# A four-layer graph network on one core: nine of 25 destination tiles get no adjacency and are summed by row gathers and one-hot products

## The chip, the core and the metric

The kernel runs on one core of one Trainium2 chip. The metric is the time of one execution on the device in microseconds (us), less is better. The five engines are called TensorE (PE in the profile; its weight loads PEld), VectorE (DVE), ScalarE (ACT), GpSimd (POOL) and SyncE (SP), which issues most of the DMAs.

## The reference, cut to what matters

There are N = 3125 nodes with 256 features and E = 53125 edges (50000 random ones and a loop for every node), sorted by destination. Four layers follow one another; each sums over the edges that arrive at a node, adds its input and normalises.

```
edge_index = stack([src, dst])
# layer 0: h = x @ W; deg = segment_sum(1, dst) + 1; norm = dinv[src] * dinv[dst]
#          out = relu(segment_sum(h[src] * norm, dst) + h * dinv**2 + b)
x = layernorm(x + L0(x))
# layer 1: agg = segment_sum(x[src] * edge_weight, dst); out = agg @ W_rel.T + b_rel + x @ W_root.T
x = layernorm(x + L1(x, edge_weight))
# layer 2: four heads of attention, a softmax over the edges of each destination
x = layernorm(x + L2(x))
# layer 3: out = relu(segment_sum((x @ W)[src] * edge_weight, dst) + b)
x = layernorm(x + L3(x, edge_weight))
```

## The kernel before

**Tiles.** The nodes are NT = 25 tiles of 128; the last holds 53. Every destination tile gets two dense adjacency matrices, sources by destinations: `ac`, the counts in bf16, used at once by layer 0, and `aw`, the weights in fp32 (1.6 MB for a tile), which is stored in `adjacency` in HBM and read back in layers 1 and 3. The random sources of a tile's some 2200 edges lie in all 25 source tiles, so that a matrix is [128, 25, 128].

**Prologue.** The edges are loaded, brought into a table of 16-edge rows (`edge_rows` in HBM), degrees are counted, and each node's row of `x @ W0` times `dinv` is split into three bf16 parts, `y0p` (semaphore `b_p3` counts the tiles that are done). SP issues its DMAs in order; among them are the `source_nodes` stores (L337, L339) in runs of 20 bytes.

**Layer 0, one tile per step `t`.** POOL's `edge_rows` gathers the tile's edges (one indirect DMA of 32 rows, one for each panel of four destinations), TensorE's `turn_fields` turns them, ScalarE's `digits` copies them to SBUF, VectorE makes one-hots of the sources (L801), of the destinations (L804) and three weighted ones (L809). TensorE's `adjacency(i, q)` multiplies them, eight quads `q` per tile (L1198, L1205); ScalarE's `counts` writes `ac` and VectorE's `add_weights` (L822) adds into `aw`. Then `aggregate` (L1213) multiplies `ac` with `y0p`: 25 blocks by three parts, 75 products of 256 columns, into `out_banks[t % 2]`, which three start products (L1251) had filled with the node's own row. The two banks alternate, so the sum of tile t (`sums0`, L839 on) may be taken during step t + 1. Each tile then passes `normalise` (L832, L833), `turn_x_next` (L1222), `relate` (L1231: the products with both weights of layer 1) and ScalarE's copy to `ybuf` (L553), one stage per step. VectorE makes the one-hots of the next tile in the second half of a step.

**Layers 1 and 3.** `dense(t)` (L1285; in layer 1 also `first_dense`, L1237, and `last_dense`, L1300; in layer 3 the first blocks ahead of time, L1451) multiplies the 25 blocks of the tile's weights with `ybuf` in fp32, while SP loads the next tiles (`load_a`, L345) into four slots. A slot's next load waits until its tile is done. Layer 1 adds two products per tile for the rows of the attention table (L1309).

**Layer 2.** 84 groups of 640 edges; for each, POOL gathers five times 128 rows of `attention_rows` (L483); VectorE, ScalarE and TensorE work out the softmax by windows of 48 destinations.

**Loops.** How many passes over edges a tile needs is worked out on the chip (`nswb`, from the fullest panel), and the steps are loops over it (`Fori`). Engines wait on counting semaphores; `sem_inc(held, 1)` stands behind some waits.

## Time and profile before

| | us |
|---|---|
| median of 3 runs | 1743.56 |
| lowest and highest | 1742.60 and 1746.69 |
| span of the profiled execution | 1741.4 |
| PE, DVE, ACT, POOL busy | 1579.5, 1180.5, 511.6, 520.9 |

The span runs from the first to the last instruction. In the page's 40 slices of 43.5 us the stages can be told by VectorE's digits: the prologue up to about 96 us, layer 0 up to 574, layer 1 up to 861, layer 2 from 871 to 1417, the rows of layer 3 up to 1484, layer 3 to the end.

```profile
## 2 busy tenths in 40 slices
PE   5879999999999999999868888888888879999998
DVE  9789999999997322122269999999999978211111
POOL 0032121221210200000077777777777700000000
PEclk9989999999999999999969999999999989999999
```

### The profile page before, as it was taken

The numbers are of one execution on the slowest core, as the hardware profiler recorded it, in microseconds if no ns is written. First come the engines' busy times: TensorE is split into PE (matmuls) and PEld (weight loads), VectorE is DVE, ScalarE is ACT, GpSimd is POOL, SyncE is SP. The second block draws the span as 40 slices with busy tenths as digits, with TensorE's granted clock in tenths as the row PEclk, the third lists the DMA queues.
The fourth block names the chain that finished last, engine by engine and source line by source line (L and its number), as shares of the span: only waits on it lengthen the run. The fifth ranks groups of instructions, "written<-read, shape, count | busy, mean of one in ns | idle before, by whom it ended". The sixth has DMA issues, their size and how long they took to land.

```text
span 1741.4 us, 37805 instructions
## 1 busy us (share of the span) xinstructions
PE 1579.5 (91%) x13731; PEld 1287.7 (74%) x13731; DVE 1180.5 (68%) x2739; ACT 511.6 (29%) x996; POOL 520.9 (30%) x540
## 2 busy tenths in 40 slices
PE   5879999999999999999868888888888879999998
PEld 4668787878877888888646666666666657888887
DVE  9789999999997322122269999999999978211111
ACT  0532322223222000000245555555555545000000
POOL 0032121221210200000077777777777700000000
PEclk9989999999999999999969999999999989999999
DMA  8912122122225244443144444444444441544440
GB/s 216 62 43 116 80 99 99 81 117 81 114 83 234 79 163 133 155 161 127 57 107 112 112 113 112 113 112 112 113 114 113 111 129 39 196 167 165 165 163 11
DMA packets 81220, 203.71 MB, mean 117 GB/s; under 512 B 42635, under 2 KB 57327, under 8 KB 71439
## 3 DMA queue, kind: packets, MB, share of 16 engines
q1 hardware_dynamic: 60047, 141.94, 26.0%
q0 software_dynamic: 20992, 59.37, 13.0%
q8 instruction: 113, 1.85, 0.4%
q14 instruction: 68, 0.56, 0.1%
HBM read 153.00 MB, written 53.57 MB: 119 GB/s over the span
## 4 chain that ended last, share of the span: by engine, by line
PE 59%; POOL 15%; DVE 11%; issue 11%; DMA 2%; ACT 1%; DVEq 0%; POOLq 0%; SPq 0%; ACTq 0%
PE bank L1285 29%; POOL ring L483 15%; PE bank L1213 10%; PE bank L1205 5%; PE bank L1198 3%; PE bank L1231 2%; PE bank L1397 2%; DMA ring<-attention_rows,work 2%; DVE work L809 1%; PE bank L1309 1%; DVE big L822 1%; PE bank L1149 1%; PE bank L1222 1%; PE bank L1115 1%; ACT work L608 1%
## 5 line engine op out<-in xcount | busy, mean ns | idle before, releaser
L483 POOL DMA_INDIRECT ring<-attention_rows,work x420 | 398.5, 949 | 149.2 <-issue 144.3
L1285 PE MATMUL bank<-big 128*128 128x256 f32 x1164 | 254.6, 379 | 0.0
L1285 PE MATMUL bank<-big,ring 128*128 128x256 f32 x1150 | 251.0, 379 | 0.0
L1397 PE MATMUL bank<-work,ring 128*65 128x48 f32 x3360 | 236.7, 231 | 12.7 <-ACT work L608 12.0
L1285 PEld LDWEIGHTS bank<-big 128*128 128x128 f32 x1164 | 220.2, 190 | 29.9 <-ACT big L632 0.4
L1397 PEld LDWEIGHTS bank<-work,ring 128*65 128x65 f32 x3360 | 225.9, 146 | 21.2 <-ACT work L608 19.4
L1285 PEld LDWEIGHTS bank<-big,ring 128*128 128x128 f32 x1150 | 217.6, 190 | 29.1
L1213 PE MATMUL bank<-big 128*128 128x256 bf16 x1875 | 209.0, 273 | 0.9
L1213 PEld LDWEIGHTS bank<-big 128*128 128x128 bf16 x1875 | 181.5, 98 | 25.3 <-ACT big L526 4.6
L608 ACT ACTIVATE work<-work 128x960 f32<-128x960 f32 x84 | 161.7, 1925 | 84.3 <-DVE work L1027 81.3
L822 DVE SCALAR_TENSOR_TENSOR big<-big,ring,bank 128x400 f32<-128x400 f32 x200 | 125.3, 628 | 34.1 <-PE bank L1205 27.2
L809 DVE TENSOR_TENSOR work<-work,ring 128x1600 bf16<-128x1600 bf16 x156 | 147.8, 986 | 0.0
L1205 PE MATMUL bank<-work 128*128 128x100 bf16 x2400 | 144.8, 209 | 0.0
L1096 DVE TENSOR_TENSOR u<-bank,bias 128x256 f32<-128x256 f32 x25 | 10.6, 425 | 193.7 <-PE bank L1285 193.7
L531 ACT ACTIVATE std<-mv,epsc 128x1 f32<-128x1 f32 x100 | 29.4, 294 | 345.1 <-DVE mv L828 344.5
L1380 PE MATMUL bank<-ident 128*32 128x512 bf16 x420 | 129.2, 408 | 0.0
L1372 PEld LDWEIGHTS bank<-ident,work 96*128 96x128 f32 x336 | 44.8, 193 | 107.5 <-DVE work L1008 105.3
L1205 PEld LDWEIGHTS bank<-work 128*128 128x128 bf16 x2400 | 122.7, 98 | 0.0
L1372 PE MATMUL bank<-ident,work 96*128 96x96 f32 x336 | 58.8, 298 | 64.8 <-DVE work L1008 64.5
L526 ACT CAST big<-bank 128x400 bf16<-128x400 f32 x200 | 96.6, 496 | 51.5 <-PE bank L1198 48.8
L446 POOL DMA_INDIRECT ring<-edge_rows,cur x26 | 24.8, 955 | 285.3 <-PE bank L1185 284.9
L994 DVE TENSOR_TENSOR work<-work,bank 128x960 f32<-128x960 f32 x84 | 96.2, 1145 | 1.3 <-issue 0.6
(220 smaller groups left out, 2050.4 us busy)
## 6 DMA issues: line engine op xcount, KB each, us to landing
adjacency<-big SPq DMA_DIRECT2D x25, 1600.0 KB, 5.1
ring<-adjacency SPq DMA_DIRECT2D x25, 1600.0 KB, 7.1
big<-adjacency SPq DMA_DIRECT2D x25, 1600.0 KB, 7.3
ring<-attention_rows,work POOLq DMA_INDIRECT x420
edge_rows<-edge_list SPq DMA_DIRECT2D x1, 4983.0 KB
x_sb<-in_x SPq DMA_DIRECT2D x1, 3072.0 KB
out_x<-xnT SPq DMA_DIRECT2D x24, 128.0 KB, 4.4
work<-attention_rows SPq DMA_DIRECT2D x168, 1.1 KB
```

The costliest lines, as they stand in the source:

```text
L483: G.indirect_dma_start(out=rows[0:EP, s, c, 0:ZG], out_offset=None, in_=ztab[:, :], in_offset=bass.IndirectOffsetOnAxis(ap=idx[:, g, c:c + ...
L526: S.copy(ac[:, :, q * QUAD * PAN:(q + 1) * QUAD * PAN], cnt_banks[q % 2][:, 0:NT * QUAD * PAN].rearrange("p (b d) -> p b d", b=NT)).then_i ...
L608: S.activation(prob[:, k % 2, :, :], val[:, k % 3].rearrange("p a c -> p c a"), ACT.Exp).then_inc(y["prob_ready"], 1)
L809: ins = V.tensor_tensor(oh[h][2][:, j], oh[h][1], repeated(digs[h][:, W1 + j], NT * PAN), ALU.mult)
L822: V.scalar_tensor_tensor(out=part, in0=part, scalar=keep[:, bass.ds(r, 1)], in1=w_banks[q % 2][:, 0:NT * QUAD * PAN].rearrange("p (b d) -> ...
L994: V.tensor_tensor(val[:, k % 3].rearrange("p (h w) c -> p h w c", h=H), pen[:, k % 3].unsqueeze(1).to_broadcast([EP, H, WIN, KC]), lg.rear ...
L1205: ins = mm(w_banks[b][:, 0:NT * QUAD * PAN].rearrange("p (b d) -> p b d", b=NT)[:, :, cols], lo[:, g, :, m], wtd[:, j, g, :, m].rearrange( ...
L1213: ins = mm(out_banks[t % 2][:, 0:D], ac[:, b, :], y0p[:, b, j, :], start=False, stop=False, skip_group_check=True)
L1285: ins = mm(bank[:, 0:D], slots[s][:, b, :], ybuf[:, b, :], start=(b == 0), stop=(b == NT - 1), skip_group_check=True)
L1372: ins = mm(mb_bank[:, j * 2 * WIN:(j + 1) * 2 * WIN], mg[:, j:j + 1].to_broadcast([2 * WIN, P]), ident[0:2 * WIN, 0:2 * WIN], start=True, ...
L1380: mm(bank[0:32, :].rearrange("p (a b) -> p a b", a=4), ident16[:, 0:32], columns, start=True, stop=True, skip_group_check=True)
L1397: ins = mm(sum_banks[k % 3][0:FH, h * WIN:(h + 1) * WIN], rows[0:EP, s, c, h * FH:(h + 1) * FH], prob[:, k % 2, c, h * WIN:(h + 1) * WIN], ...
```

## The change

Tiles 1, 4, 7, ..., 22 (eight of them, `SPARSE`) and the last, short tile 24 get no adjacency; the other 16 (`DENSE`) go through the steps as before, so layer 0 has 16 steps and layers 1 and 3 have 16 dense sums each. The edges of a sparse tile are cut in 18 chunks of 128 (8 for the last tile), in blocks of 10 and 8: 17 blocks and 152 chunks per layer. For each block SP loads the edges' sources and destinations (in layers 1 and 3 the weights too) as lists, POOL gathers 128 source rows per chunk from a table in HBM (`rows_layer0`, 1536 bytes a row; `rows_layer1`, `rows_layer3`, 1024 bytes), VectorE makes one-hots of destinations against the tile's 128 nodes (in layers 1 and 3 times the weight), and TensorE adds one-hot times rows: three bf16 products a chunk in layer 0, one fp32 product in layers 1 and 3.

The tables are new: SP stores `y0p` in five parts at the end of the prologue and each tile's rows in layers 1 and 3; six more stores keep the edge lists. In layer 0 there is now one bank for dense tiles and one for sparse ones, and one buffer for gathered rows and for one-hots; in layers 1 and 3 two of each. A block stands behind nearly every dense tile (`after0`: one per step, two in the last; `after1`: from step 1, two in steps 7 and 12; `after3`: from step 3, two in 5, 8, 11 and 13). Tiles leave layers in another order (`order0`, `order1`, `order3`). `nswb` now also covers the longest sparse tile. `edge_rows` copies its column of `cur` and `panel` first, since the tile is worked out in a register.

```
+    SPARSE = list(range(1, NT - 1, 3))
+    DENSE = [t for t in range(NT - 1) if t not in SPARSE]
+    halves = [Block(t, at, cnt, WIDE) for t in SPARSE for at, cnt in ((0, TEN), (TEN, WIDE - TEN))]
+    short = [Block(NT - 1, 0, SHORT, SHORT)]
+    blocks = short + halves + short + halves + halves + short
+    after0 = placed(0, [(k, 1 + (k == ND - 1)) for k in range(ND)])
+    after1 = placed(LAYER, [(k, 1 + (k in (7, 12))) for k in range(1, ND)])
+    after3 = placed(2 * LAYER, [(k, 1 + (k in (5, 8, 11, 13))) for k in range(3, ND)])
...
SP:
+            for table, whole, pad in ((esrc, src_e, pad_i[:, 0, :]), (edst, dst_e[:, 0:COLS], pad_i[:, 1, :]), (ew, w_e, pad_w)):
+                sp.dma_start(table[0:CAP].rearrange("(p e) -> p e", p=P), whole).then_inc(s_elist, 16)
+                sp.dma_start(table[CAP:CAP + P * WIDE].rearrange("(p e) -> p e", p=P), pad).then_inc(s_elist, 16)
...
+            for b in range(0, NT, 5):
+                sp.wait_ge(b_p3, b + 5)
+                sp.dma_start(y0tab[b * P:(b + 5) * P, :].rearrange("(t p) f -> p t f", p=P),
+                             y0p[:, b:b + 5].rearrange("p t j f -> p t (j f)")).then_inc(rows_stored[0], 16)
...
+            def lists(q):
...
+                    sp.wait_ge(chunk_done, two_blocks_back(nswb, q, r))
...
POOL:
+            def edge_rows(col, i):
                 pool.wait_ge(c_T, i + 1)
                 pool.wait_ge(c_next, i + 1)
                 pool.sem_inc(held, 1)
+                G.tensor_copy(cur1, cur[:, bass.ds(col, 1)]).then_inc(pool_col, 1)
+                G.tensor_copy(panel1, panel[:, bass.ds(col, 1)]).then_inc(pool_col, 1)
...
+            def gathers(q):
+                b, j = blocks[q], q % 2
                 with pool.Fori(0, nswb) as r:
+                    pool.wait_ge(lists_loaded[j], lists_here(nswb, q, r))
+                    if q >= LAYER:
+                        pool.wait_ge(chunk_done, two_blocks_back(nswb, q, r))
+                    pool.sem_inc(held, 1)
+                    for c in range(b.cnt):
+                        s = slot_of(q, c)
+                        if q < LAYER:
+                            pool.wait_ge(chunk_done, slot0_free(nswb, q, c, r))
...
+            edge_rows(DENSE[0], 0)
+            pool.wait_ge(rows_stored[0], 16 * (NT // 5))
+            pool.wait_ge(s_wz, 1)
+            for k in range(ND):
...
+                for q in after0[k]:
+                    gathers(q)
...
+            G.memset(big1[:, SPARSE_WORDS:], 0.0)
+            pool.wait_ge(rows_stored[1], 16 * NT)
+            for q in range(LAYER, 2 * LAYER):
+                gathers(q)
...
+            pool.wait_ge(chunk_done, blocks_done(nswb, 2 * LAYER - 1))
+            pool.sem_inc(held, 1)
+            G.memset(big1[:, 0:SPARSE_WORDS], 0.0).then_inc(acc_clear, 1)
...
VectorE:
+            def hots0(q):
+                b, pairs = blocks[q], blocks[q].cnt // PAIR
+                with dve.Fori(0, nswb) as r:
+                    relative(q, r, rel0, dst_l0)
+                    dve.wait_ge(chunk_done, rounds_done(nswb, q, r))
+                    V.tensor_tensor(hot0[:, 0:pairs], iota2.unsqueeze(1).to_broadcast([P, pairs, P, PAIR]),
...
+            def hots1(q):
+                b, j = blocks[q], q % 2
+                with dve.Fori(0, nswb) as r:
+                    relative(q, r, rel1[j], dst_l1)
+                    dve.wait_ge(chunk_done, two_blocks_back(nswb, q, r))
+                    for c in range(b.cnt):
+                        ins = V.tensor_scalar(hot1[:, j, c, :], iota_w[:], rel1[j][:, c:c + 1], w_l1[j][:, c:c + 1],
+                                              ALU.is_equal, ALU.mult)
...
+                for m in summed0(k - 1):
+                    normalise(e0, m, x_sb[:, order0[m], :])
+                for m in summed0(k)[:-1] if k < ND else summed0(k):
+                    sums0(m, k)
+                if k < ND:
+                    hots0(after0[k][0])
+                    sums0(summed0(k)[-1], k)
+                for m in summed0(k - 2):
+                    residual(m)
...
-                    dve.wait_ge(gathered[k % SLOTS], 16 * KC * uses(r, k))
+                    dve.wait_ge(gathered[k % SLOTS], 16 * KC * uses(r, k) + nswb * landed_before[k % SLOTS])
...
TensorE:
+            def scatter0(q):
...
+                with pe.Fori(0, nswb) as r:
+                    pe.wait_ge(hot_made, nswb * q + r + 1)
+                    for c in range(b.cnt):
+                        pe.wait_ge(rows_landed[slot_of(q, c)], nswb * (16 * slot_uses[q][c]) + r * 16 + 16)
+                        for j in range(3):
+                            ins = mm(sparse_bank[:, 0:D], hot0[:, c // PAIR, :, c % PAIR], rows0[:, c, j * D:(j + 1) * D],
...
+                        pe.wait_ge(rows_landed[s], landed)
+                        mm(bank[:, 0:D], hot1[:, q % 2, c, :], rows1[:, s, :], start=False, stop=False,
...
+            for k in range(ND + 3):
+                if k < ND:
+                    if k >= 1:
+                        pe.wait_ge(e0["u"], place0[DENSE[k - 1]] + 1)
+                    init0(dense_bank, DENSE[k])
...
+                relating, turning = summed0(k - 2), summed0(k - 1)
+                for m in relating[:1]:
+                    relate(m)
...
+                for m in turning[:1]:
+                    turn_x_next(e0, m, order0[m])
+                if k < ND:
+                    scatter0(after0[k][0])
+                for m in relating[1:]:
+                    relate(m)
...
```

## Rows read from the trace of the kernel before

**Rows 1.** The page's first line: the span and the instructions.
```profile
span 1741.4 us, 37805 instructions
```
**Rows 2.** Busy time by stage: layer 0, layer 2. The first line names the columns.
```profile
core 0: us, PE busy (x) PEld busy (x) DVE busy (x) ACT busy (x) POOL busy (x), PEclk, DMA share, GB/s
140.00:560.00 420.00, 409.02 (x4996) 338.04 (x4997) 385.55 (x587) 114.09 (x302) 82.77 (x88) 1.00 0.26 107
870.00:1417.00 547.00, 457.71 (x4788) 337.28 (x4788) 492.03 (x1262) 280.13 (x338) 398.46 (x420) 0.93 0.42 108
```
**Rows 3.** Timeline of one step: start us, us, engine, line, what, count, idle before.
```profile
284.21 0.50 PE L1251 MATMUL bank<-big,ident 128*128 128x256 bf16 x3
...
290.53 0.98 DVE L804 TENSOR_TENSOR work<-ring 128x1600 bf16<-128x1600 bf16 x1
...
291.61 8.36 PE L1213 MATMUL bank<-big 128*128 128x256 bf16 x75
...
299.81 1.88 PE L1231 MATMUL bank<-w_rr,xnT 128*128 128x512 f32 x4
...
301.11 0.15 DVE L832 RECIPROCAL rstd<-std 128x1 f32<-128x1 f32 x1
...
301.63 0.48 DVE L839 SCALAR_TENSOR_TENSOR u<-bank,dinv,bias 128x256 f32<-128x256 f32 x1
...
302.17 0.50 PE L1251 MATMUL bank<-big,ident 128*128 128x256 bf16 x3
...
303.16 0.39 DVE L847 TENSOR_TENSOR x_sb<-bank,x_sb 128x256 f32<-128x256 f32 x1
```
**Rows 4.** Prologue: SP's last long store, POOL after its first gather, two stretches.
```profile
45.65 39.12 SPq L339 DMA_DIRECT2D source_nodes<-in_src  x1
...
93.06 0.24 POOL L450 TENSOR_SCALAR cur<-cur 32x1 int32<-32x1 int32 x1 [20.07 <-DMA ring<-edge_rows,cur]
...
0.00:96.00 96.00, 62.53 (x609) 50.40 (x609) 79.49 (x195) 31.61 (x80) 8.86 (x15) 1.00 1.02 126
72.00:84.00 12.00, 9.05 (x45) 6.66 (x43) 9.50 (x28) 8.48 (x23) 0.99 (x1) 1.00 1.39 9
```
**Rows 5.** Timeline: the fields turned in the first step, and the second step's start.
```profile
110.14 0.41 PE L1185 MATMUL bank<-ident,ring 32*128 32x32 bf16 x5
...
123.08 0.49 PE L1251 MATMUL bank<-big,ident 128*128 128x256 bf16 x3
```
**Rows 6.** Timeline: first product of layer 1's second tile, last sum of layer 1.
```profile
573.88 10.96 PE L1285 MATMUL bank<-big 128*128 128x256 f32 x50
...
861.00 0.42 DVE L932 TENSOR_TENSOR u<-bank,x_sb 128x256 f32<-128x256 f32 x1 [7.56 <-PE bank L1300]
```
**Rows 7.** The chain that ended last: start us, us, what; in layers 1 and 3.
```profile
597.19 10.79 PE bank L1285 x50
...
1483.29 251.08 PE bank L1285 x1162
```
**Rows 8.** Two gathers of layer 2, one's landing in the chain, an adjacency store.
```profile
999.42 0.95 POOL L483 DMA_INDIRECT ring<-attention_rows,work  x1 [0.30 <-issue]
1000.67 0.94 POOL L483 DMA_INDIRECT ring<-attention_rows,work  x1 [0.30 <-issue]
...
1020.66 3.53 DMA ring<-attention_rows,work
...
adjacency<-big SPq DMA_DIRECT2D x25, 1600.0 KB, 5.1
```
**Rows 9.** Timeline: POOL and DVE instructions that overlap.
```profile
98.36 1.34 POOL L446 DMA_INDIRECT ring<-edge_rows,cur  x1 [0.18 <-issue]
...
273.48 1.22 DVE L801 TENSOR_TENSOR work<-ring 128x2048 bf16<-128x2048 bf16 x1
273.87 0.92 POOL L450 TENSOR_SCALAR cur<-cur 32x1 int32<-32x1 int32 x1 [1.67 <-DMA ring<-edge_rows,cur]
...
584.90 5.43 POOL L465 MEMSET big<- 128x6400 f32 x1 [56.44 <-PE bank L1285]
...
586.53 3.94 DVE L833 TENSOR_SCALAR x_sb<-u,mv,rstd 128x256 f32<-128x256 f32 x1
```

719 lines of the change are left out of this document (476 added, 243 removed).

## The prediction

> **What bounds the kernel now.** I read the page's span first [rows 1], then the table by stage [rows 2], then one period of layer 0 in the timeline [rows 3]. The four layers are limited by different things.
>
> Layer 0 (96 to 574 us) repeats every 17.96 us, once for each of 25 tiles: the start products of one step stand at 284.21, of the next at 302.17 [rows 3]. Follow two chains. TensorE goes from 284.21 through eight quads to 291.61, then 8.36 us of aggregation, 1.88 us of `relate`, a turn, and the next start. VectorE begins the one-hots at 290.53, is through at 301.11, normalises, sums, and releases that start. Both close at the same moment: the stage is balanced, 409 us of TensorE and 386 of VectorE busy in 420 [rows 2].
>
> Layers 1 and 3 are fp32 products back to back: 10.79 us for a tile of 25 blocks, and the whole end is one piece of 251.08 us [rows 7] (581 block products, two records each). One block product costs 251.08/581 = 0.432 us. Layer 2 (547 us [rows 2]) isn't touched; its gathers follow one another every 1.25 us [rows 8].
>
> **One pass or two.** All sparse work stands in loops over `nswb`. From the reference's inputs: the eight sparse tiles have at most 137 granules of 16 edges (144 fit 18 chunks), the last tile has 55 (64 fit), no panel has over 6. So `nswb` stays 1.
>
> **Layer 0, the period.** Twenty-five periods become 16, each with one block of 8 or 10 chunks (152 chunks in 17 blocks). Let D be the moment VectorE ends its one-hots. Two things become serial that weren't: the dense bank is now single, so TensorE's next start waits for `sums0` of this step, and `scatter0` stands ahead of that start and waits for `hots0`, which VectorE makes only after D.
> - Odd steps (block of 10, a sparse tile completed before): normalise 0.52 (301.11 to 301.63 [rows 3]), one more `sums0` 1.53 (301.63 to 303.16), list subtraction and one-hot of 1280 elements 1.35 (from 0.98 for 1600 elements, plus about 0.5 for the small instruction and two waits), 30 products of 8.36/75 = 0.111 us: 3.34, a second `relate` 1.88 and its wait: start at D+8.8.
> - Even steps (8 chunks): 1.04 + 1.25 + 2.7 + a second turn 0.4 (the one between 299.81 + 1.88 and 302.17): start at D+5.4.
> - From the start to the next D: 6.3 (284.21 to 290.53) + 10.6 (290.53 to 301.11).
> That gives 25.7 and 22.3, mean 24.0. Loop branches, a register wait ahead of every chunk and queueing behind POOL have no row; I bound them by 0 and 4 and take 1. Period 25.0. TensorE's own work is 22.6 (7.4 + 8.36 + 1.56 x 2.3 + 3.3), which would be the period if nothing were serial.
>
> POOL has to fit too: a gather every 1.25 us [rows 8] makes 11.3 us a step, and `edge_rows` about 8 (seven operations near 0.9, as L450's 0.92 [rows 9], and 1.7 of waiting): 19 of 25. Gathers start when the block before is consumed (D+4), the tenth lands 3.5 us after its issue (1020.66, 3.53 [rows 8]), near D+19; needed at D+27. Hidden with 8 us to spare; a store of the adjacency beside it takes some of that.
>
> **Layer 0, its ends.** Before it, `source_nodes` holds SP's queue to 84.8 (45.65 + 39.12 [rows 4]) and the engines are full of tiny packets: DMA share 1.39 at 9 GB/s between 72 and 84 us. The first row gather lands only at 93.06. The new store of `rows_layer0` (4.9 MB) stands behind all that, and POOL waits for its last part before its second `edge_rows`. An adjacency store (1.6 MB) lands in 5.1 us [rows 8], so 16 us at best; at the 126 GB/s of the first stage [rows 4] 39; I take 22 and its end at 118. Eight us of `edge_rows` later, at 126, TensorE can turn the fields that it turned at 110.14 before [rows 5]: +16, in which 3 us for six list stores and VectorE's dozen small instructions are counted. The first scatter and sum add 6. Start of step 1: 145 instead of 123.1 (+22; bounds +6 and +40).
>
> After it: D of step 15 is 145 + 14 x 25 + 16.9 = 512. Then the two last blocks and `first_dense` by the same prices: block 15 done at D+7, relate +1.9, 16 blocks at 0.432 (+6.9), the last 8 gathers free from D+4, landed D+17, scattered D+17.5; relate, 5 blocks, turns, three more relates with their ACT copies and 4 blocks: first dense product at D+33 = 545. Before: 573.88 [rows 6]. **Layer 0: -29** (period 22.6 and 28 give -63 and +13).
>
> **Layer 1.** Before, 573.88 to the last sum at 861.00 [rows 6] is 287.1: 24 x 10.79 [rows 7] + 28.1 for 25 tiles' inputs and turns. After: 15 x 10.79 = 161.9, 152 chunks x 0.432 = 65.7, the same 28.1, zero products and loops 6: 261.7. The first gathers can't start before the last row of layer 1 is stored: 4 + 10 + 2.5 against 11 of dense cover costs 5; later waits 3. So 269.7. Tail: two tiles are late together, and POOL clears 7760 words (5.43 us per 6400 [rows 9]: 6.6, mostly beside the last tiles' rows): +2. **Layer 1: -15.** The nine adjacency loads fewer save nothing by themselves: no product of the one piece of layer 3 [rows 7] waits for a load, and layer 1 is built alike.
>
> **Layer 2.** VectorE's `logits_sum` waits get one more register term, 84 times; no row. 0 to +4, I take +1. The stage between layers 2 and 3 gets only the stores of `rows_layer3`, on SP, where nobody waits for them before layer 3: 0.
>
> **Layer 3.** Before 251.1 [rows 7]. 43 blocks are done ahead in either. After: 357 x 0.432 = 154.2 + 65.7 + 6 = 225.9. But 152 gathers at 1.25 are 190 us, with only two blocks of buffer, and each block's lists and gathers may start only when the block two before is consumed. Laying the 17 blocks out by these prices gives 4 us of stalls at 1.25, 12 at 1.4, 20 at 1.5. I take 1.4: VectorE's 9 one-hots per block and the 1.6 MB loads get in the way. 240: **layer 3: -11**.
>
> **The shared port.** The trace shows POOL and VectorE waiting for each other: beside a memset of 584.90 + 5.43 a `tensor_scalar` that takes 0.41 took 3.94 and ended with it, and L450 (0.24 when free, 93.06 [rows 4]) took 0.92 and ended about when VectorE's one-hot of 273.48 did [rows 9]. The gather at 98.36 took 1.34 instead of 0.94, with the same two one-hot operations beside it. In layer 2 the gather's period stays 1.25.
> The Trainium skill, "SBUF — State Buffer", section "Who interferes with whom", says the second port pair of VectorE is GpSimd's only one and is locked exclusively for an instruction, by `tensor_scalar` in a two-port mode among others, and that DMAs issued by GpSimd starve meanwhile. `hots1` is made of nothing but `tensor_scalar`. By that rule 9 of them hold up each block's gathers in layers 1 and 3; with the page's own 3.1 us for a DMA issue that is overlapped instead of 0.62 the change would lose. Rows 9 agree for memset and small operations; for gathers no run here shows it beyond the 1.34.
>
> **Sum.** -29 - 15 + 1 - 11 = -54. The profiled execution's 1741.4 lies 2 us under the median of 1743.56, which carries over: 1743.56 - 54 = **1690 us**.
>
> **Rivals.**
> - *Full overlap* (0.12): waits shorter than laid out, period 22.6, TensorE's sum. Layer 0 gives -63: 1656. For: before, TensorE is 97% busy in this stage. Against: hots0 after D can't start earlier.
> - *Longer hand-over* (0.20): each of the new waits costs some 0.5 more, period 28: layer 0 +13, in all 1732. For: three hand-overs between VectorE and TensorE per step where there was one.
> - *Dear gathers* (0.12, slower): POOL's gather is held up in layers 1 and 3 behind `hots1`. At 1.75 us each layer 3 stalls 48 us (+22) and layer 1 13 (-8); with layer 0 the sum is near -15; from about 1.8 on the change costs time, and at 1.9 (layer 1 +11, layer 3 +44) it is 1771. Against: layer 2's steady 1.25 beside a VectorE that is 90% busy.
> - *Dear gathers and longer hand-over, both small* (0.05): within 0.3% of before, about 1743.
> - *Two passes* (0.01): excluded by the counts above; every adjacency would be built twice, over 2000.
> - The forecast, 0.50, with its own range 1665 to 1714.
>
> **Numbers.** 1690. Range 1650 to 1735, from full overlap to the longer hand-over with its bound; outside are mostly the dear gathers. Within 0.3% is about what a measurement of this kernel can tell from no change. Faster: 0.50 + 0.12 + 0.20 = 0.82; same 0.05; slower 0.13.
>
> **What would show it.** Start products of layer 0 every 25 us, in pairs near 23 and 27, with TensorE idle ahead of the scatter products for VectorE's one-hot. Fields of step 0 turned near 126. First full dense product near 545. In layer 3 POOL's gathers nearly unbroken, every 1.4 us, products waiting after the steps with two blocks. Wrong if the gather's period passes 1.7, if layer 0's period passes 28, or if TensorE waits for landed rows in layer 0.

## The result

The changed kernel takes 1673.92 us (median of 4 runs, 1669.85 to 1676.1) against 1743.08 for the kernel before: a ratio of 0.9601, with a 95% interval of 0.9581 to 0.962, or 69 us less. The prediction was 1690 (1650 to 1735), 54 us less. The profiled execution took 1676.1, its span is 1674.3 against 1741.4 [rows 1].

Busy time by stage of the changed kernel: the steady part of layer 0, layer 1, the end of layer 3. Columns as in rows 2.

```profile
core 0: us, PE busy (x) PEld busy (x) DVE busy (x) ACT busy (x) POOL busy (x), PEclk, DMA share, GB/s
140.00:470.00 330.00, 300.49 (x3429) 247.48 (x3427) 259.80 (x423) 78.69 (x198) 248.13 (x224) 0.99 0.48 158
524.00:804.00 280.00, 262.25 (x1210) 224.70 (x1208) 124.34 (x441) 25.95 (x113) 156.57 (x156) 0.98 0.50 161
1430.00:1667.00 237.00, 226.73 (x1032) 195.51 (x1030) 91.09 (x313) 7.44 (x25) 145.21 (x152) 0.99 0.56 183
```

Layer 0 was balanced between TensorE and VectorE before, each 92 to 97% busy [rows 2]. Now TensorE is busy 91% of it, VectorE 79%, and POOL, once at 20%, is at 75%: a third engine has come up close. Layer 2 is the same: 525.1 us from its first gather to its last in both kernels.

One step of layer 0 in the changed kernel (timeline, columns as in rows 3; L1569 starts a bank, L1063 is VectorE's first one-hot for the next tile, L1538 the dense aggregation, L1125 the block's one-hots `hot0`, L1583 the scatter products):

```profile
281.85 0.49 PE L1569 MATMUL bank<-big,ident 128*128 128x256 bf16 x3
...
288.05 0.99 DVE L1063 TENSOR_TENSOR work<-ring 128x1600 bf16<-128x1600 bf16 x1
...
289.14 8.36 PE L1538 MATMUL bank<-big 128*128 128x256 bf16 x75
...
298.62 0.15 DVE L1091 RECIPROCAL rstd<-std 128x1 f32<-128x1 f32 x1
...
301.24 0.83 DVE L1125 TENSOR_TENSOR ring<-ring 128x1280 bf16<-128x1280 bf16 x1 [0.20 <-DVE ring L1117]
...
302.27 3.45 PE L1583 MATMUL bank<-ring 128*128 128x256 bf16 x30 [2.10 <-DVE ring L1125]
305.56 1.88 PE L1556 MATMUL bank<-w_rr,xnT 128*128 128x512 f32 x4
307.28 0.49 PE L1569 MATMUL bank<-big,ident 128*128 128x256 bf16 x3
```

A step of 25.43 us, from 281.85 to 307.28. TensorE has nothing to do from 300.17 to 302.27: `hot0` stands behind VectorE's one-hots, which end at 298.70, and behind the sums. The wait for `hot0` is 2.1 and 1.2 us in turn over layer 0, 16 waits and 27.2 us in all. Dense tiles start at 138.50, 164.95, 186.93, 212.40 and so on to 472.11: alternately every 25.45 and 22.0 us, 23.83 on average (333.61 in 14 steps). Sixteen such steps stand where 25 of 17.96 stood [rows 3].

The start of layer 0 (timeline; L1510 turns the edge fields, L634 opens the second `edge_rows`, which waited for the stored rows):

```profile
103.36 0.82 PE L1569 MATMUL bank<-big,ident 128*128 128x256 bf16 x3
...
111.08 2.26 POOL L634 COPY ring<-cur 32x1 int32 x1 [12.01 <-DMA rows_layer<-big]
...
118.72 0.37 PE L1510 MATMUL bank<-ident,ring 32*128 32x32 bf16 x5 [1.97 <-POOL ring L649]
...
138.50 0.49 PE L1569 MATMUL bank<-big,ident 128*128 128x256 bf16 x3
```

The fields were turned at 110.14 and the second step began at 123.08 before [rows 5].

Both ends of layer 1 (timeline; L1656 dense products, L667 gathers, L697 the clearing on POOL, L1214 a cast and L1232 the last sum on VectorE, L709 the first gather of layer 2):

```profile
524.35 10.96 PE L1656 MATMUL bank<-big 128*128 128x256 f32 x50
...
532.88 0.95 POOL L667 DMA_INDIRECT big<-rows_layer,big  x1 [22.96 <-issue]
...
550.84 9.44 PE L1656 MATMUL bank<-big,ring 128*128 128x256 f32 x43
...
796.07 6.56 POOL L697 MEMSET big<- 128x7760 f32 x1 [12.90 <-PE bank L1604]
...
797.04 5.61 DVE L1214 CAST work<-edf 128x4 bf16<-128x4 f32 x1 [1.48 <-ACT edf L806]
...
803.84 0.42 DVE L1232 TENSOR_TENSOR u<-bank,x_sb 128x256 f32<-128x256 f32 x1 [0.38 <-issue]
...
817.99 0.95 POOL L709 DMA_INDIRECT ring<-attention_rows,work  x1 [15.36 <-issue]
```

Layer 1 takes 279.5 us from 524.35 to its last sum, against 287.1 [rows 6]. It loses at both ends: the first block's rows come so late that the next dense product starts 26.5 us after the first (10.96 of products and some 6 of scatter and inputs fill it), and the last sum stands behind a cast of four elements that takes 5.61 us, as long as POOL's memset runs.

In layer 3 TensorE stands before the scatter products that follow a step with two blocks (timeline; L507 issues a load of 1.6 MB of the adjacency):

```profile
1556.06 3.62 PE L1604 MATMUL bank<-big 128*128 128x256 f32 x16
1556.14 0.33 SPq L507 DMA_DIRECT2D big<-adjacency  x1
...
1563.33 1.57 PE L1604 MATMUL bank<-big 128*128 128x256 f32 x4 [3.66 <-DMA big<-rows_layer,big]
```

Where the time went, by stage (start and end read from the timelines):

| stretch | before | changed | difference | predicted |
|---|---|---|---|---|
| to the second step of layer 0 | 123.1 | 138.5 | +15.4 | +22 |
| second step to layer 1's first full dense product | 450.8 | 385.9 | -64.9 | -51 |
| layer 1 to its last sum, and on to the first gather of layer 2 | 297.2 | 293.6 | -3.6 | -15 |
| from that gather to the end of the stage before layer 3 | 612.2 | 612.9 | +1 | +1 |
| layer 3 | 251.1 | 236.3 | -15 | -11 |
| all | | | -67 | -54 |

### The profile page after: what moved, and what is told of

Read it like the earlier page. It is cut to its first block, busy times and chain, and to the rows that moved or that the text cites. A ratio compares the mean times of both kernels' runs of the same rounds, so it can differ in the third digit from the quotient of the medians.

```text
span 1674.3 us, 36559 instructions
## 1 busy us (share of the span) xinstructions
PE 1451.5 (87%) x12043; PEld 1166.7 (70%) x12043; DVE 1163.9 (70%) x2961; ACT 482.0 (29%) x906; POOL 1007.3 (60%) x1011
## 3 DMA queue, kind: packets, MB, share of 16 engines
q1 hardware_dynamic: 87087, 110.47, 22.3%
## 4 chain that ended last, share of the span: by engine, by line
PE 38%; DVE 19%; POOL 19%; issue 15%; DMA 6%; ACT 2%; DVEq 1%; SPq 0%; POOLq 0%; ACTq 0%
POOL ring L709 16%; PE bank L1656 15%; PE bank L1604 7%; DVE work L1068 5%; PE bank L1583 3%; PE bank L1530 2%; POOL big L667 2%; PE bank L1757 2%; DMA big<-rows_layer,big 2%; DMA ring<-attention_rows,work 2%; DVE big L1081 2%; DVE work L1063 2%; PE bank L1665 1%; PE bank L1474 1%; PE bank L1523 1%
## 5 line engine op out<-in xcount | busy, mean ns | idle before, releaser
L709 POOL DMA_INDIRECT ring<-attention_rows,work x420 | 398.4, 949 | 143.0 <-issue 139.1
L667 POOL DMA_INDIRECT big<-rows_layer,big x304 | 289.6, 953 | 288.9 <-issue 268.7
L663 POOL DMA_INDIRECT ring<-rows_layer,ring x152 | 196.3, 1291 | 66.1 <-issue 44.0
L1656 PE MATMUL bank<-big,ring 128*128 128x256 f32 x800 | 177.0, 382 | 0.0
L1656 PEld LDWEIGHTS bank<-big,ring 128*128 128x128 f32 x800 | 153.7, 192 | 21.6
L1604 PE MATMUL bank<-big 128*128 128x256 f32 x608 | 143.9, 390 | 17.8 <-DMA big<-rows_layer,big 17.8
L1656 PE MATMUL bank<-big 128*128 128x256 f32 x664 | 145.9, 379 | 0.0
L1604 PEld LDWEIGHTS bank<-big 128*128 128x128 f32 x608 | 114.8, 194 | 39.1 <-DMA big<-rows_layer,big 23.3
L1656 PEld LDWEIGHTS bank<-big 128*128 128x128 f32 x664 | 126.1, 190 | 17.6 <-ACT big L877 0.4
L1538 PE MATMUL bank<-big 128*128 128x256 bf16 x1200 | 133.8, 273 | 0.5
L1538 PEld LDWEIGHTS bank<-big 128*128 128x128 bf16 x1200 | 116.1, 98 | 16.1 <-ACT big L758 2.8
L1081 DVE SCALAR_TENSOR_TENSOR big<-big,ring,bank 128x400 f32<-128x400 f32 x128 | 80.0, 629 | 53.2 <-PE bank L1530 49.1
L1068 DVE TENSOR_TENSOR work<-work,ring 128x1600 bf16<-128x1600 bf16 x102 | 96.5, 988 | 0.0
```

Source lines behind the costliest of these rows:

```text
L663: G.indirect_dma_start(out=rows0[:, s, :], out_offset=None, in_=y0tab[:, :], in_offset=bass.IndirectOffsetOnAxis(ap=src_l0[j][:, c:c + 1], ...
L667: G.indirect_dma_start(out=rows1[:, s, :], out_offset=None, in_=(y1tab if q < 2 * LAYER else y3tab)[:, :], in_offset=bass.IndirectOffsetOn ...
L709: G.indirect_dma_start(out=rows[0:EP, s, c, 0:ZG], out_offset=None, in_=ztab[:, :], in_offset=bass.IndirectOffsetOnAxis(ap=idx[:, g, c:c + ...
L1068: ins = V.tensor_tensor(oh[h][2][:, j], oh[h][1], repeated(digs[h][:, W1 + j], NT * PAN), ALU.mult)
L1081: V.scalar_tensor_tensor(out=part, in0=part, scalar=keep[:, bass.ds(r, 1)], in1=w_banks[q % 2][:, 0:NT * QUAD * PAN].rearrange("p (b d) -> ...
L1538: ins = mm(dense_bank[:, 0:D], ac[:, b, :], y0p[:, b, j, :], start=False, stop=False, skip_group_check=True)
```

## The experiments

Every profile here is of one run. "Period" is the mean over the 14 steps of layer 0 from the second dense tile to the last.

| kernel | second step | period | layer 1's first dense product | from there to layer 2's first gather | median us | ratio to before (95%) |
|---|---|---|---|---|---|---|
| changed | 138.5 | 23.83 | 524.4 | 293.6 | 1673.9 | 0.9601 (0.9581 to 0.962) |
| e0, the same again | 137.2 | 24.41 | 531.4 | 290.7 | 1676.6 | 0.9607 (0.9587 to 0.9626) |
| e1 `hot0` first | 139.8 | 23.80 | 529.2 | 290.0 | 1674.1 | 0.9579 (0.9542 to 0.9615) |
| e2 gaps | 139.7 | 25.42 | 548.0 | 292.0 | 1696.4 | 0.9706 (0.9683 to 0.9728) |
| e3 lists first | 141.1 | 23.94 | 528.0 | 286.0 | 1677.3 | 0.9608 (0.9583 to 0.9632) |
| e4 clearing split | 139.6 | 23.99 | 528.9 | 284.2 | 1674.7 | 0.9574 (0.9542 to 0.9605) |
| e5 = e1 + e2 | 135.7 | 22.68 | 503.0 | 288.4 | 1651.4 | 0.9456 (0.944 to 0.9473) |
| e6 joints | 132.5 | 23.90 | 518.8 | 279.1 | 1664.7 | 0.954 (0.9517 to 0.9562) |
| e7 = e5 + e6 | 131.8 | 22.73 | 500.4 | 281.0 | 1641.8 | 0.939 (0.9366 to 0.9415) |
| e8 = e7, one gap | 131.4 | 22.32 | 493.2 | 280.8 | 1637.9 | 0.9394 (0.9378 to 0.941) |
| e9 = e7, copying spread | 128.7 | 22.70 | 496.5 | 280.8 | 1638.4 | 0.9402 (0.9384 to 0.9421) |
| e10 = e7 without layer 3's rows | 132.1 | 22.72 | 500.2 | 279.0 | 1625.0 | 0.9321 (0.9304 to 0.9338) |
| e11 = e8 + e9 | 127.6 | 22.30 | 489.8 | 278.0 | 1633.0 | 0.9366 (0.9342 to 0.9389) |

My theory of the period was that the hand-over `hot0` to scatter sets it. The first two runs test that, and what stands next in line.

**e1, the block's one-hots at the head of the step.**

```diff
+                    hots0(after0[k][0])
                     with dve.Fori(0, nswb) as r:
...
                 if k < ND:
-                    hots0(after0[k][0])
                     sums0(summed0(k)[-1], k)
```

> Edit: in layer 0 the one-hots of the sparse block (`hot0`) are made at the head of the step, ahead of the dense tile's adjacency, instead of behind its one-hots and sums (valid where each tile has one round, as here). In the changed kernel TensorE stood 2.10 us before the scatter products of 15 of the 16 steps, released by that `hot0` instruction. Theory A, the hand-over alone sets the period: init of the dense bank then comes every 21.9 us on average (alternately 23.4 and 20.0 to 20.9, some of the gain lost because VectorE starts its first weighted sum 1 us later) instead of 23.83; layer 0 is 23 to 31 us shorter and the kernel takes 1643 to 1651 us against 1674. Theory B, GpSimd is the next bound (edge rows 8 us and 9 gathers of 1.25 us on average is 19.3, plus a hold of 5.8 us in most steps is 22.5 to 25): the period stops at 22.8 or more, TensorE now waits for landed rows, and the kernel takes 1655 to 1665 us.

The waits for `hot0` (27.2 us in all; the 2.10 us that I had for 15 of the 16 steps hold for every second one) are gone, and nothing is gained that the timing shows: the period is 23.80 instead of 23.83. Timeline of a step with ten chunks in e1:

```profile
291.98 6.79 POOL L663 DMA_INDIRECT ring<-rows_layer,ring  x1 [0.30 <-issue]
...
299.34 2.47 PE L1583 MATMUL bank<-ring 128*128 128x256 bf16 x21
302.32 0.50 PE L1583 MATMUL bank<-ring 128*128 128x256 bf16 x3 [0.52 <-DMA ring<-rows_layer,ring]
...
304.74 0.51 PE L1583 MATMUL bank<-ring 128*128 128x256 bf16 x3 [0.65 <-DMA ring<-rows_layer,ring]
```

The last three rows come one by one, at the gathers' own pace, because one gather before them took 6.79 us instead of 0.95 (a hold, from here on). In the changed kernel such a hold is seen in 10 places in layer 0 and delays TensorE once, by 1.8 us in the first step; in e1 it comes in every step from the second on, and TensorE waits for landed rows 21 times between 140 and 480 us, 14.8 us in all. Theory B names the right mechanism; its size (1655 to 1665) was too kind. The slack that I had called 8 us was used up by the hold.

**e2, gaps in VectorE's one-hots.**

```diff
+            def one_hot_lo(h, i=None):
+                V.tensor_tensor(oh[h][0], numbers(P), repeated(digs[h][:, LO], P), ALU.is_equal).then_inc(c_lo, 1)
+                if i is not None:
+                    dve.wait_ge(c_lo, i * 2 + (h + 1))
...
+                else:
+                    ins.then_inc(c_wt, 1)
+                    if h == 1:
+                        dve.wait_ge(c_wt, i * 4 + (2 * h + j + 1))
...
-                        one_hot_code(1)
-                        one_hot_lo(1)
+                        one_hot_code(1, i + 1)
+                        one_hot_lo(1, i + 1)
```

> Edit: in layer 0 VectorE waits for the completion of each of the five one-hot instructions of the second half before it starts the next, so that its unbroken stretch (some 4.8 us of 2-input tensor_tensor on SBUF operands) is broken by four gaps of about 0.2 us. In the changed kernel a GpSimd instruction takes 6.3 to 6.9 us instead of 0.95 about once in every second step, and each time it ends where this stretch of VectorE ends. Theory A, the stretch holds the port that GpSimd's instruction needs and any gap lets it in: the longest GpSimd instruction of layer 0 drops to under 3 us, none of over 5 us is left. Theory B, the hold is of another origin (the DMA's descriptors, an instruction fetch): the 6 to 7 us instructions stay. Both: the hold is hidden behind GpSimd's slack, so the time doesn't fall; VectorE's own stretch is 1 us longer per step, the time is within -3 and +15 us of 1674.

The hold itself, first in the changed kernel (timeline; L1063, L1060 and L1068 are one-hots, `tensor_tensor` operations with both inputs in SBUF, the last five of which are the second half; L1081 is `add_weights`, with one input in PSUM; the last one-hot ends at 298.70):

```profile
288.95 1.22 DVE L1060 TENSOR_TENSOR work<-ring 128x2048 bf16<-128x2048 bf16 x1
289.18 1.81 POOL L663 DMA_INDIRECT ring<-rows_layer,ring  x1 [0.30 <-issue]
290.08 0.62 DVE L1081 SCALAR_TENSOR_TENSOR big<-big,ring,bank 128x400 f32<-128x400 f32 x1
...
292.07 1.89 DVE L1068 TENSOR_TENSOR work<-work,ring 128x1600 bf16<-128x1600 bf16 x2
292.73 6.79 POOL L663 DMA_INDIRECT ring<-rows_layer,ring  x1 [0.30 <-issue]
293.87 0.98 DVE L1063 TENSOR_TENSOR work<-ring 128x1600 bf16<-128x1600 bf16 x1
...
295.91 2.79 DVE L1068 TENSOR_TENSOR work<-work,ring 128x1600 bf16<-128x1600 bf16 x3
```

and in e2:

```profile
199.81 2.94 POOL L664 DMA_INDIRECT ring<-rows_layer,ring  x1 [0.30 <-issue]
...
200.94 0.98 DVE L1066 TENSOR_TENSOR work<-ring 128x1600 bf16<-128x1600 bf16 x1
...
201.96 1.23 DVE L1061 TENSOR_TENSOR work<-ring 128x2048 bf16<-128x2048 bf16 x1
```

Every hold of 6.3 to 6.9 us is gone; the longest is 3.04, a shade over the 3 expected. In both kernels POOL's instruction ends 0.8 us after the end of the one-hot operation that closes an unbroken train of them: 299.52 after 298.70, and 202.75 after 201.93, where the added wait leaves 0.04 us free before the next. What ends the train need not be a pause. At 298.70 VectorE had already begun its next instruction (L1091, of another form), and the gather of 289.18 ends at 290.99, 0.8 us after the one-hot of 288.95, though `add_weights` follows that at once (20 gathers of the changed kernel between 140 and 460 us end so, 0.77 to 0.83 us after such a one-hot). So the 6.79 us are the rest of one one-hot operation and the six behind it, the last of the first half included, and a gap or an operation of another form lets POOL in. That is theory A for the cause. For the time I was wrong: by the ratios (0.9706 against 0.9601) it is 18 us more, not at most 15. VectorE's five operations take 5.32 us instead of 4.82, not 1 us more, `hot0` is later by it, and TensorE's granted clock is 0.92 to 0.97 in most stretches of 50 us of layer 0 where it was 1.00; the period went from 23.83 to 25.42. How much of the 1.6 us is the clock's no run separates.

**e5, both edits together.**

> Edit: both edits of e1 and e2 together, `hot0` at the head of the step and a wait for completion after each one-hot instruction of the second half. In e1 TensorE no longer waited for `hot0` but for landed rows, and GpSimd had a hold of 6.79 us in every step; in e2 the longest hold was 3.0 us, but TensorE stood longer before the scatter products and its granted clock fell to 0.92 to 0.97 in most stretches of 50 us. Theory A, holds on GpSimd are the bound of e1: with both edits the holds are 3 us, TensorE waits for rows under 5 us in all of layer 0, dense tiles follow each other every 22.0 to 22.8 us and the first dense product of layer 1 comes at 500 to 512 us; the kernel takes 1650 to 1662 us. Theory B, the steps of e1 are bound by the gathers as such (a slot is free only when its last rows are multiplied): the period stays at 23.4 to 24 us, 1672 us or more.

Theory A holds in all its numbers: period 22.68, first dense product at 503.0, 1651.4 us. The first edit gains nothing alone, the second costs 18 us alone, and together they gain 25 (1651.4 against e0's 1676.6 on the same chip). TensorE now goes from `relate` straight into the scatter products (timeline of e5), and the table of the stretch shows it busy 95% at full clock:

```profile
334.62 0.50 PE L1578 MATMUL bank<-big,ident 128*128 128x256 bf16 x3
335.03 3.45 PE L1592 MATMUL bank<-ring 128*128 128x256 bf16 x30
338.32 1.88 PE L1565 MATMUL bank<-w_rr,xnT 128*128 128x512 f32 x4
...
140.00:480.00 340.00, 322.65 (x3666) 266.97 (x3663) 282.68 (x458) 83.70 (x212) 238.15 (x238) 1.00 0.52 170
```

**e8, one gap in place of four.**

```diff
+                if h == 1:
+                    ins.then_inc(c_lo, 1)
...
                         one_hot_code(1)
                         one_hot_lo(1)
+                        dve.wait_ge(c_lo, i + 2)
                         for j in range(3):
                             weighted(i + 1, 1, j)
```

> Edit: e7 with one wait for completion in VectorE's stretch of the second half (behind its second one-hot instruction) in place of four. In e5 and e7 the holds on GpSimd are 1.9 and 2.9 us, longer than one piece of VectorE's stretch (0.9 to 1.2 us), and TensorE stood 0.9 us in 14 steps before a transpose that waits for VectorE. Theory A, GpSimd's instruction gets in at the first gap: with one gap the holds are at most 4 us, VectorE is 0.5 us earlier in each step, the first dense product of layer 1 comes at 490 to 500 us instead of 500.4 and the kernel takes 1633 to 1642 us. Theory B, it needs more than one gap (2.9 us is two or three pieces): holds of 5 us or more are back, TensorE waits for landed rows as in e1, the dense product comes at 508 us or later and the kernel takes 1648 us or more.

The longest hold is 4.08 us (230.55 to 234.63; the operation before the one gap of that step ends at 233.80: again 0.8 later). Period 22.32, layer 0 shorter by 7 us in the profile. The ratio, 0.9394, can't be told from e7's 0.939, so the gain in the profile is shown for layer 0 only.

**e0, the changed kernel again.** Layer 0 ended 4 us later in e3 and e4, whose layer 0 is the changed kernel's, so I looked at how it scatters.

> The changed kernel itself once more, beside the next three on one chip, to see how far layer 0 alone scatters from run to run (its first dense product came at 524.35 us in the first profile, and at 528.0 and 528.9 in two kernels whose layer 0 is the same). Both theories: ratio to before 0.958 to 0.962. Theory A, the scatter is one of the start (TensorE's clock and the first step, 138.5 or 139.6 to 141.1 at the second dense tile) and of single steps: the first dense product lies between 523 and 530 us here. Theory B, the placement of code did it: it lies at 524.4 within 0.5 us.

The first dense product came at 531.4, a microsecond beyond theory A's bracket and 7 behind the first profile. The same step in both (timeline; the changed kernel first, then e0, then e0's table by stretch):

```profile
207.39 3.45 PE L1583 MATMUL bank<-ring 128*128 128x256 bf16 x30 [2.14 <-DVE ring L1125]
```
```profile
204.82 5.10 PE L1583 MATMUL bank<-ring 128*128 128x256 bf16 x30 [2.10 <-DVE ring L1125]
```
```profile
204.00:206.00 2.00, 1.18 (x6) 0.85 (x7) 1.90 (x5) 0.00 (x0) 0.69 (x1) 0.71 0.01 2
206.00:208.00 2.00, 2.00 (x11) 1.35 (x10) 0.46 (x2) 0.29 (x1) 1.01 (x3) 0.50 0.00 0
```

The same 30 products after the same wait of 2.1 us for `hot0` take 3.45 us in one run and 5.10 in the other, where TensorE's granted clock fell to 0.50, its lower level of 1.2 GHz, as it began them. What the engine had done before was the same by the rows: 8.36 us of products, 1.88, a turn, a start, then the wait. So the wait for `hot0` has a second price, which some steps of some runs pay, here 1.65 us. In e5, where the wait is gone, every stretch of layer 0 from 140 us on has a clock of 1.00, and its five runs lie within 3.9 us (1648.94 to 1652.83) where the changed kernel's lie within 7.6 in e0.

**e3, the lists of layer 1 first.**

```diff
             load_a(slots1[1], 1, 1)
+            lists(after1[1][0])
             sp.wait_ge(c_oh, nswb * (2 * ND) + 2)
...
-                for q in after1.get(k + 1, []):
+                for q in after1.get(k + 1, []) if k else []:
                     lists(q)
```

> Edit: at the start of layer 1 the edge lists of its first sparse block are loaded ahead of two adjacency loads, the last y1 stores and the load of the node indices, instead of behind them. In the changed kernel the first gather of layer 1 starts at 532.9 us, 5 us after its lists were issued and 9 us after the last y1 store was, and the first sparse block ends at 549.9 where TensorE alone would have ended it at about 540.5. Theory A, the lists' place in the queue sets the first gather: it starts 5 to 7 us earlier (right behind the last y1 store's landing), the first sparse block ends 5 to 8 us earlier, and the kernel takes 1666 to 1669 us. Theory B, the loads of 1.6 MB next to the gathers set when rows land (8.6 us was seen against 2.9): the gathers start earlier but the block ends less than 2 us earlier, 1672 to 1674 us.

The first gather comes 1.9 us after the first dense product instead of 8.5, and the third tile's products start 19.6 us after it instead of 26.5: theory A within layer 1. The time doesn't show it (0.9608, and 1677.3 us where I expected at most 1674): in its profile layer 0 was 3.7 us longer than in the changed kernel's, and so was the stretch from layer 2's first gather to the end. The scatter of e0 is as large as the gain.

**e4, the clearing cut in two.**

```diff
-            pool.wait_ge(chunk_done, blocks_done(nswb, 2 * LAYER - 1))
+            pool.wait_ge(chunk_done, blocks_done(nswb, 2 * LAYER - 2))
             pool.sem_inc(held, 1)
-            G.memset(big1[:, 0:SPARSE_WORDS], 0.0).then_inc(acc_clear, 1)
+            G.memset(big1[:, 0:TEN * D], 0.0)
+            G.memset(big1[:, 2 * TEN * D:2 * TEN * D + TEN * P], 0.0)
+            pool.wait_ge(e1["split"], 5 * NT)
+            pool.sem_inc(held, 1)
+            G.memset(big1[:, TEN * D:2 * TEN * D], 0.0)
+            G.memset(big1[:, 2 * TEN * D + TEN * P:SPARSE_WORDS], 0.0).then_inc(acc_clear, 1)
```

> Edit: the clearing of the 7760 words of rows and one-hots at the end of layer 1 is cut in two: one half behind the last block but one, the other behind VectorE's last split of a layer-1 tile. In the changed kernel that memset starts on GpSimd at 796.07 and takes 6.56 us, and VectorE's cast of 4 elements that starts at 797.04 takes 5.61 us instead of 0.16; the last sum of layer 1 comes behind it. Theory A, the memset holds VectorE: without it there the last sum starts 5 to 6 us earlier, the first attention gather too (at 812 to 813 instead of 818.0), and the kernel takes 1668 to 1669 us. Theory B, something else is as late (the scatter products, the stores of z): the first gather moves by under 2 us, 1672 to 1674 us.

Timeline of e4:

```profile
807.80 2.23 POOL L701 MEMSET big<- 128x2560 f32 x1 [18.46 <-DVE ring L1219]
...
813.07 0.97 POOL L714 DMA_INDIRECT ring<-attention_rows,work  x1 [1.81 <-issue]
```

No cast takes over 0.2 us there any more, though a copy beside the second clearing still takes 1.91 us (808.18) for 0.20. From the last scatter product to the first gather of layer 2 it is 14.5 us (798.6 to 813.1) instead of 22.1 (795.9 to 818.0). Theory A at its place; the ratio, 0.9574, is 5 us under the changed kernel's, within the interval, and the median of 1674.7 us is not the 1668 to 1669 expected. Layer 3 alone, the same in all kernels here but e10, takes between 236.2 (e8) and 242.6 us (this one) in their profiles, so that single gains of this size drown in the total.

**e6, three joints at once**: e3, e4, and POOL's wait for the stored rows behind the second `edge_rows` instead of ahead of it.

```diff
-            pool.wait_ge(rows_stored[0], 16 * (NT // 5))
             for k in range(ND):
...
                              if following > this else this, nswb * k + r + 1)
+                if k == 0:
+                    pool.wait_ge(rows_stored[0], 16 * (NT // 5))
```

> Edit: three moves at the joints, and layer 0's steps left as they are: e3's (lists of layer 1 first, 7 us shorter from the first dense product to the third in its profile), e4's (clearing cut in two, 7.5 us shorter from the last scatter product to the first attention gather), and GpSimd's wait for the layer-0 rows moved behind the second tile's edge rows, which don't need them. Theory A, the three gains are in series on the path: the first step of layer 0 is 5 to 8 us shorter (init of the second dense tile at 131 to 134 us instead of 138.5), from there to the first attention gather it is 14 us less, and the kernel takes 1650 to 1658 us, 18 to 24 us under the changed kernel on the same chip. Theory B, what is gained at one joint is waited for at the next (the DMA queues, the clock after it): under 8 us gained, 1667 us or more.

Each local number is as theory A had it: second step at 132.5, 279.1 us from the first dense product of layer 1 to layer 2's first gather (14.6 less than in the changed kernel, 11.7 less than in e0). The median fell by 12 us on the same chip (0.954 against 0.9607), less than the 18 to 24 expected. The profiled run was the fastest of its five, 7 us under the median; what the others lost, and where, I can't say without their profiles.

**e7, all of it.**

> Edit: everything of e1 to e4 and the moved wait of e6 together. Theory A, the gains add: e6's 20 us and e5's 12 to 22 us give 1630 to 1642 us. Theory B, layer 0 stays bound by GpSimd's gathers and only the joints gain: 1650 to 1660 us.

1641.8 us: at the upper end of theory A. e5's gain of 25 and e6's of 12 add to 37; measured 35 (0.939 against 0.9607 is 38 by the ratio).

**e9, the copying of the source nodes spread over layer 0.**

```diff
-            sp.dma_start(src_all[:, 0:FULL, :], src[0:FULL * EP * KC].rearrange("(g p k) -> p g k", p=EP, k=KC)).then_inc(
-                s_srcs, 16)
...
             for k in range(ND):
...
                 lists(after0[k][0])
+                lo, hi = FULL * k // ND, FULL * (k + 1) // ND
+                sp.dma_start(src_all[:, lo:hi, :], src[lo * EP * KC:hi * EP * KC].rearrange(
+                    "(g p k) -> p g k", p=EP, k=KC)).then_inc(s_srcs, 16)
```

> Edit: e7 with the copying of the source nodes (55 us of SyncE's queue in pieces of 20 bytes, ahead of the stores of layer 0's rows) cut into 16 parts that follow the list loads of layer 0's 16 steps, 3.4 us of the queue in each. In the changed kernel five stores of rows (960 KB each) start together at 91.6 us and the last lands at 111. Theory A, the queue's hold sets the first gathers: the row stores go out as their tiles are ready, the last lands at 104 to 108 us, init of the second dense tile comes 3 to 6 us earlier than in e7 (131.8), and the kernel takes 1636 to 1640 us on e7's scale. Theory B, the first step is bound by the edge rows and by the last tile of rows anyway, and 3.4 us of tiny pieces in each step only delay lists and adjacency stores: init of the second dense tile moves by under 1.5 us, 1640 to 1650 us.

The second step starts at 128.7, 3.1 us before e7's, and stays so to the first dense product (3.9). The last store of rows lands at 101.2, 9.9 us before e7's, so most of that is not on the path. Each of the 16 parts holds SP's queue for 0.6 to 1.7 us, 11.0 us in all, not for the 3.4 that I had divided out of 55: cut up, the copying holds the queue less. The ratio (0.9402) can't be told from e7's.

**e11, e8 and e9 together.**

> Edit: e7 with both e8's single wait and e9's spread copying of the source nodes. In the profiles of e8 and e9 the first dense product of layer 1 came 7.2 and 3.9 us earlier than in e7, while the medians of the three kernels were within what the timing tells apart (0.9390, 0.9394, 0.9402 of before). Theory A, both gains are real and the medians only scatter: the first dense product comes at 487 to 492 us and the ratio is 0.932 to 0.937 (1626 to 1634 us). Theory B, what is gained in layer 0 is given back later (the hand-over to layer 1, TensorE's clock): the ratio stays at 0.938 to 0.941 (1636 to 1642 us).

Theory A: the first dense product at 489.8, a ratio of 0.9366, though its interval still overlaps those of e7 and e8. This is the fastest complete kernel found, some 42 us under the changed one (0.9366 against 0.9607). It is valid as long as each tile has one round: with two, by the order of the waits (no run has two), `hot0` at the head of the step would wait for products that stand behind VectorE's own next one-hots.

**e10, layer 3 without its rows.**

```diff
-            for q in range(2 * LAYER, 3 * LAYER):
-                gathers(q)
...
-                        pe.wait_ge(rows_landed[s], landed)
+                        if e is not e3:
+                            pe.wait_ge(rows_landed[s], landed)
```

> Left out: layer 3's gathers, and the waits for their rows; the products run on what lies in the buffers, so the output is not the reference's. Otherwise e7. In e7 as in the changed kernel TensorE stood 10.4 us in layer 3 before scatter products, released by gathered rows that landed. Theory A, these landings are all that layer 3 loses: it is 9 to 12 us shorter from its first dense product to the end and the kernel takes 1630 to 1633 us on e7's scale. Theory B, the adjacency loads (16 of 1.6 MB) or VectorE's one-hots are next and as late: under 4 us gained.

From its first dense product with weights in `ring` to its last product layer 3 takes 217.9 us instead of e7's 237.1: 19.2 less, twice what theory A gave. The waits for landed rows are 10.4 us of that. The rest is in the same products (grouped by line and shape, e7 first; L1672 and L1671 dense, L1620 and L1619 scatter):

```profile
L1672 PE MATMUL bank<-big,ring 128*128 128x256 f32 x400 | 91.7, 392 | 0.0
L1620 PE MATMUL bank<-big 128*128 128x256 f32 x304 | 72.5, 391 | 10.5 <-DMA big<-rows_layer,big 10.4
```
```profile
L1671 PE MATMUL bank<-big,ring 128*128 128x256 f32 x400 | 87.5, 379 | 0.0
L1619 PE MATMUL bank<-big 128*128 128x256 f32 x304 | 67.9, 379 | 0.0
```

4.2 and 4.6 us, 8.8 in all: e7's granted clock in this stretch is 0.96, e10's 1.00. With the waits the clock's share goes too; the edit takes the gathers away together with the waits, so which of the two held the clock down is not shown. e7's profile is one of the dear ones: e8 and e9, whose layer 3 is e7's, take 232.9 and 233.8 us for the same stretch at a clock of 0.99, so that e10 is 15 to 16 us shorter than these, some 10 of waits and 5 of clock. By the timed ratios the gain is 12 us (0.9321 against 0.939); from layer 2's last gather to the first use of its sums e10's profile had 25.5 us, e7's 22.8. With no gathers TensorE is busy 221.97 of 222 us, so neither the adjacency loads nor VectorE's one-hots are next.

## Why the prediction was right, and where it wasn't

The direction, the stages and most mechanisms held, but that the sum came within 15 of the 69 us is in part luck. By the profiles layer 0 gained 20.5 us more than forecast (6.6 of them at its start) and layer 3 some 4 more, and layer 1 gained 11 less, which hid half of the first error.

- **Two hand-overs made serial set layer 0's period**: right. The layout gave 25.7 and 22.3 us; measured 25.45 and 22.0. The microsecond that I added for loops and register waits isn't there: 30 scatter products with ten waits take 3.45 us, where 30 x 0.111 is 3.34. Fourteen steps of it were the largest miss: 16 us. The layout's own hand-over is right to 0.3 us: D comes 16.9 us after the start, as laid out, and the next start 8.6 after D, laid out as 8.8.
- **Start, 145**: measured 138.5. The stores were mis-sized: POOL was let go at 111.1, not 118, as the five stores (4.9 MB) went out from 91.6 on and had all landed at 110.5: 256 GB/s from 91.6 to 111, where the 126 of the slow end would have taken 39 us. The first start product was 7 us later than before, where I had 3. Then 7.6 us of `edge_rows`, as said.
- **Hand-over to layer 1**: 52.2 us from the last start product to the first dense product, predicted 49.9.
- **Layer 1, 269.7**: measured 279.5. The term that failed is the waits, 8 in the sum. The first block cost about 10 (e3: the lists stood behind other loads, 7 of it), the later ones 1.3, and the clearing held VectorE for 5.6 just before the last sum (e4). I had the memset in the sum, from rows 9 even its power over VectorE, but "mostly beside the last tiles' rows", when the last sum was behind it.
- **Layer 2, +1**: measured nothing that stands out (525.1 us from first to last gather in both).
- **Layer 3, 240**: 236.3. The size was about right (225.9 and the 12 of stalls for a period of 1.4 make 238, not 240; measured stalls are 10.2), the place too, and the mechanism wrong. The gathers' period is not 1.4: it is 1.25 in the middle, as in rows 8. Two of the stalls, 3.7 us each after steps with two blocks, are landings beside a load of 1.6 MB (the two links of the chain that ended last are 7.27 and 7.18 us long; the median landing is 2.9; the loads run from 1503.99 to 1511.45 and from 1556.14 to 1563.47). That the load delays the rows is read from these times; no run moves it away. The other 2.8 us, between 1631 and 1636, are rows of a late block that land one by one at the gathers' own pace. e10 shows that the gathers and their waits, with the clock, are all that layer 3 loses.
- **Gathers in layer 0, hidden with 8 us to spare**: the verdict held, the margin didn't. Ten holds of 5.8 us in 16 steps make 22.6 us a step out of the 19 that I had for POOL (9.5 gathers a step, not the 9 that I priced, add 0.6 more). It is my third sign of being wrong, rows that TensorE waits for in layer 0, and it was seen once, for 1.8 us. As the wait for `hot0` was as long, it showed only when e1 took that away.
- **Full overlap (0.12)**: its period of 22.6 was out of reach for the reason given, `hot0` after D. With that and the holds gone, e5 reached 22.68.
- **Longer hand-over (0.20)**: no; the hand-overs cost what their rows say. Its own price was too high as well: three hand-overs with 0.5 us more each make 26.5, not 28.
- **Dear gathers (0.12)**: no in layers 1 and 3. Of the 304 gathers there 61 overlap a `tensor_scalar` one-hot (L1135), and they take 0.95 us in the middle and 1.08 at most. The rule of the Trainium skill, "SBUF — State Buffer", section "Who interferes with whom", by which they might have locked the port doesn't show for this form (fp32, 128 elements, two scalars read from SBUF).
- **The hold in layer 0** I didn't see coming, though rows 9 had its small form. The same section of the Trainium skill says that a VectorE instruction with two SBUF inputs contends with a GpSimd instruction that reads SBUF, which is what `tensor_tensor` on one-hots and a gather with its list are: here the trace agrees, with 6.79 us against 0.95. But it adds that `tensor_tensor` wasn't seen to stall DMA issue, and that the ports are held for an instruction; here a gather was held over the rest of one operation and six more, until a gap or another form followed. The measurements decide.

## What to carry to other kernels

When a wait is removed and nothing is gained, look for the resource whose slack was about as long; the two must go together (e1 gains nothing, e2 loses, and e5 gains 25 us). A wait on TensorE costs its length and, in some runs, slower products after it: in layer 3, some 10 us of waits and their gathers stood with 5 us (e8, e9) to 8.8 us (e7) of clock. Clear buffers at a moment when VectorE is idle, not when they first become free. When errors of a forecast have both signs, judge it stage by stage: the sum flatters it.

## What the runs showed of the hardware

- An indirect gather, or another small GpSimd instruction, that starts while VectorE runs `tensor_tensor` operations on SBUF operands back to back ends 0.8 us after the last of them: 6.79 us for 0.95 over the rest of one and six more, 4.08 with one wait for completion in the train, 2.94 with four. A gap of 0.04 us ends the train, and so does an operation with an input in PSUM that follows at once (1.81 us).
- A memset on GpSimd holds even a cast of four elements on VectorE: 5.61 us for 0.17.
- TensorE's granted clock fell to 0.50 over most of 30 products after a wait of 2.1 us in one run and not in another, with the same rows before it. Which of the two happens no row shows.
- The copying in 20-byte pieces held SP's queue for 55 us (36.2 to 91.2; the longest DMA 42.7). In sixteen parts behind the list loads it held it for 11.0 us in all and cost nothing that the timing shows (e9).
